# A state-space scan on one core: a\*h split per state, and element-wise work moved from VectorE to GpSimd and ScalarE

## The chip, the cores and the metric

The kernel runs on one core of one Trainium2 chip. The metric is device time in microseconds (us), the median of three runs for the kernel before. A core has five engines that run their own instruction streams in order and meet at semaphores: TensorE (PE, matrix products into the accumulator memory PSUM), VectorE (DVE), ScalarE (ACT, activation functions), GpSimd (POOL) and SyncE (SP, which here issues all DMAs).

## What is computed

The reference, cut to what matters (8 images of 48 x 48 positions, 256 channels, 512 inner channels, 16 states):

```python
xh, z = split(layernorm(x) @ W_in)
xc = depthwise_conv_3x3(xh)
dt_r, Bp, Cp = split(xc @ W_xproj)
dt  = softplus(dt_r @ W_dt + b_dt)          # 512 channels
dtN = dt @ W_dtN + b_dtN                    # 16 states
for t in range(48 * 48):                    # the scan over positions
    dA = exp(dt[t][:, :, None] * A)
    h  = dA * h + (dtN[t] * Bp[t])[:, None, :] * xc[t][:, :, None]
    y[t] = einsum('bdn,bn->bd', h, Cp[t]) + Dskip * xc[t]
y = layernorm(y) * ln_g + ln_b
x = x + (y * silu(z)) @ W_out + b_out
out = x + small_table_function(layernorm(x))   # shifts of 4-bit numbers coded one-hot
```

## The kernel before

The scan has 2304 steps, 48 for each image row, and the state is laid out as 128 partitions (a half of the channels, an image, a pair of states) by 256 channels, twice (the two states n = 0 and 1 of the pair). Of the 256 channels VectorE has 192 (`VD`) and GpSimd 64. A step on VectorE is `decay_state` (L823: one 384-wide product a\*h, both states, in place in PSUM) and then `add_input` (L835: two 192-wide operations, one per state, that add the input and write `h`). ScalarE makes a = exp(dt\*A) for two steps at a time into one of two PSUM buffers (`decay`, L616); it may refill a buffer once the step pair two pairs back is finished, so it leads VectorE by two or three steps. It makes GpSimd's share for four steps at a time (`decay_pool`, L626). Every four steps TensorE sums over the states with the C weights (`sum_states`, L470), for which it needs four finished steps from VectorE and GpSimd; `h` is a ring of eight steps, so VectorE and GpSimd in turn wait for the sum of the quad two quads back.

Around the scan lies a software pipeline over rows. While row i is scanned, row i+1 is convolved and given its dt, row i-1 is normalised, gated, projected and stored, and row i+4 is normalised and projected. The order is written out by hand: the table `SLOT` and conditions on the step `s` (0 to 47) say in which step each stage is issued on each engine, and since every engine runs in order, a stage that waits holds the scan's instructions behind it. The projections share two PSUM banks in strict turn: a stage may use a bank when the stage two turns back has been copied out.

The stages that matter here, with the step at which they stand:

- steps 8 to 12, `dt_project` on TensorE; `softplus_parts`, `softplus_exp`, `softplus_log` on ScalarE (steps 9 to 16); `finish_dt` (L875) on VectorE adds the two parts of softplus (steps 14 to 17).
- steps 9 and 10, `y_log_var` and `y_scale` (L692, L696) on ScalarE make 1/sigma of y, and `y_norm` (L902, three of 512) on VectorE applies it. TensorE transposes y (`yt`), ScalarE scales it (`scale_yn`, L733), VectorE gates it (`gate_y`, L907).
- step 22, `copy_y` (L726) on ScalarE frees `ps_y`; TensorE then runs `add_skip` (L454), a sum, two transposes of dt (L537), `dtn_project` (L544), a sum and `out_project` (L561), whose first result VectorE adds at step 27 (L921).
- steps 33 to 38, z is projected (L496), ScalarE takes tanh(z/2) of it (`gate_tanh`, L741) and VectorE makes z\*(1+tanh(z/2)) = 2 silu(z) (`make_sz`, L914); the factor 2 is taken out of W_out. Behind the last of them stands an explicit load of ScalarE's activation table for exp and ln (L795), and the first tanh has one of its own.
- steps 39 and 40, ScalarE makes 1/sigma for the last norm (L702, L706), for which VectorE waits at step 39 (L943).
- `weigh_c` (L851) spreads the C weights, three times a row, on VectorE; `ln1_apply` (L870) applies the first norm there (steps 20 to 22).

## Time and profile before

| | |
|---|---|
| median of 3 runs | 4378.39 us (4372.62 to 4378.6) |
| the profiled execution | 4383.27 us, span of its instructions 4381.5 us |
| busy: PE, DVE, ACT, POOL | 77%, 91%, 64%, 64% of the span |
| mean granted TensorE clock | 0.815 of full |
| DMA | 78.2% of 16 engines' time, 790 MB |

Busy time is an average over a row whose stretches have different limits. The chain of work that ended last says which engine was being waited for at each moment; the table by windows says how full each engine was between two such moments. An instruction's duration is longer than the time it blocks its engine, since the next may start before the last has drained; where a timeline is at hand, the distance between two starts is the price.

### The profile page before, as it was taken

How to read it: one execution, taken by the hardware profiler on the slowest of the kernel's cores; microseconds unless marked ns; L12 is line 12 of the kernel's file. 1: busy time of each engine (PE TensorE's matmuls, PEld its weight loads, DVE VectorE, ACT ScalarE, POOL GpSimd, SP SyncE). 2: the span in 40 equal slices, each digit the busy share in tenths (PEclk: the TensorE clock that was granted, in tenths of full speed). 3: DMA queues.
4: the chain of work that ended last, by engine and by line, in shares of the span. 5: the costliest groups of instructions: out<-in, count | busy, mean ns of one | idle time of the engine just before them, and what ended most of it. 6: DMA issues, size and time to landing. Idle time of an engine off the chain costs nothing.

```text
span 4381.5 us, 99554 instructions
## 1 busy us (share of the span) xinstructions
PE 3371.7 (77%) x33792; PEld 1640.6 (37%) x33792; DVE 3978.8 (91%) x10877; ACT 2811.1 (64%) x5762; POOL 2797.6 (64%) x5195
## 2 busy tenths in 40 slices
PE   5778787878787777777787878787878787777765
PEld 2334333433343333433343334333433343334322
DVE  2899999999999999999999999999999999999997
ACT  2666666666666666666666666666666666666653
POOL 0766666666666666666666666666666666666664
PEclk8778887888788878888888878887888778878876
DMA  3888788877878787878787888788877878788874
GB/s 71 198 187 191 182 186 185 191 178 183 185 184 186 180 189 182 195 179 188 184 193 177 186 185 189 179 186 187 193 182 183 186 184 186 180 189 182 187 168 105
DMA packets 300420, 789.99 MB, mean 180 GB/s; under 512 B 71301, under 2 KB 225926, under 8 KB 226182
## 3 DMA queue, kind: packets, MB, share of 16 engines
q1 hardware_dynamic: 299910, 783.62, 78.2%
q8 instruction: 268, 4.39, 0.5%
q14 instruction: 242, 1.98, 0.2%
HBM read 648.18 MB, written 96.73 MB: 170 GB/s over the span
## 4 chain that ended last, share of the span: by engine, by line
DVE 47%; PE 31%; ACT 11%; issue 8%; SPq 1%; POOL 1%; DMA 1%; DVEq 0%; ACTq 0%; POOLq 0%
DVE h L835 18%; DVE ps_a L823 13%; PE ps_y L470 6%; PE ps_s L506 6%; ACT ps_a L616 4%; PE ps_y L454 3%; PE ps_s L515 3%; PE ps_s L544 3%; PE ps_s L561 2%; PE ps_s L489 2%; PE ps_s L529 2%; PE ps_s L496 2%; DVE yn L907 2%; DVE res L949 2%; DVE y L902 2%
## 5 line engine op out<-in xcount | busy, mean ns | idle before, releaser
L616 ACT ACTIVATE ps_a<-xb,a_n 128x384 f32<-128x384 f32 x2304 | 1248.0, 574 | 1035.8 <-DVE h L835 1020.9
L835 DVE SCALAR_TENSOR_TENSOR h<-xb,db,ps_a 128x192 f32<-128x192 f32 x4608 | 1685.8, 406 | 62.6 <-DVE ps_a L823 1.4
L1142 POOL TENSOR_TENSOR mp<-ap,h 128x128 f32<-128x128 f32 x2304 | 1091.2, 474 | 520.0 <-ACT ap L626 383.6
L1152 POOL TENSOR_TENSOR h<-mp,up 128x128 f32<-128x128 f32 x2304 | 1108.1, 481 | 489.8 <-PE ps_y L470 305.5
L823 DVE TENSOR_TENSOR ps_a<-ps_a,h 128x384 f32<-128x384 f32 x2304 | 1291.6, 561 | 104.2 <-ACT ps_a L616 12.0
L1132 POOL TENSOR_TENSOR up<-xb,db 128x512 f32<-128x512 f32 x576 | 617.6, 1072 | 532.3 <-DMA xb<-xd 451.1
L470 PE MATMUL ps_y<-h,cw 64*32 64x256 f32 x18432 | 822.3, 478 | 92.9 <-DVE h L835 92.9
L626 ACT ACTIVATE ap<-xb,a_n 128x256 f32<-128x256 f32 x1152 | 519.1, 500 | 171.3 <-DMA xb<-xd 169.8
L470 PEld LDWEIGHTS ps_y<-h,cw 64*32 64x32 f32 x18432 | 322.9, 125 | 528.0 <-issue 259.5
L489 PE MATMUL ps_s<-xlnT,win 128*128 128x384 f32 x768 | 315.9, 550 | 202.1 <-ACT xh L719 152.2
L506 PE MATMUL ps_s<-xs,conv_w 96*32 96x384 f32 x4608 | 411.0, 507 | 13.6 <-ACT xc L634 11.9
L496 PE MATMUL ps_s<-xlnT,win 128*128 128x384 f32 x768 | 325.2, 568 | 117.6 <-DVE sz L914 114.6
L553 PE MATMUL ps_s<-swap,y 128*128 128x128 f32 x576 | 160.7, 434 | 200.6 <-ACT yn L733 169.3
L454 PE MATMUL ps_y<-skip_w,xc 128*32 128x128 f32 x4608 | 197.6, 325 | 136.0 <-ACT y L726 136.0
L561 PE MATMUL ps_s<-wout,yn 128*128 128x256 f32 x1152 | 289.5, 395 | 1.4 <-DVE yn L907 1.4
L529 PE MATMUL ps_s<-xp,wdt 9*128 9x384 f32 x384 | 276.5, 851 | 1.0 <-ACT xp L643 1.0
L489 PEld LDWEIGHTS ps_s<-xlnT,win 128*128 128x128 f32 x768 | 145.4, 204 | 335.8 <-ACT xh L719 204.6
L496 PEld LDWEIGHTS ps_s<-xlnT,win 128*128 128x128 f32 x768 | 155.2, 216 | 268.0 <-DVE sz L914 164.4
L506 PEld LDWEIGHTS ps_s<-xs,conv_w 96*32 96x32 f32 x4608 | 141.5, 114 | 271.2 <-issue 252.7
L561 PEld LDWEIGHTS ps_s<-wout,yn 128*128 128x128 f32 x1152 | 208.7, 191 | 76.2 <-issue 51.6
L454 PEld LDWEIGHTS ps_y<-skip_w,xc 128*32 128x32 f32 x4608 | 145.1, 129 | 198.7 <-ACT y L726 168.1
L553 PEld LDWEIGHTS ps_s<-swap,y 128*128 128x128 f32 x576 | 96.1, 211 | 322.3 <-ACT yn L733 229.2
(107 smaller groups left out, 3799.4 us busy)
## 6 DMA issues: line engine op xcount, KB each, us to landing
xb<-xd SPq DMA_DIRECT2D x576, 1024.0 KB, 7.8
xs<-xh SPq DMA_DIRECT2D x196, 192.0 KB, 8.6
xd<-dttok SPq DMA_DIRECT2D x288, 128.0 KB, 6.1
xin<-in_x_dram SPq DMA_DIRECT2D x144, 128.0 KB, 7.0
xd<-xtok SPq DMA_DIRECT2D x192, 96.0 KB
res<-in_x_dram SPq DMA_DIRECT2D x144, 128.0 KB, 7.1
out_dram<-res SPq DMA_DIRECT2D x144, 128.0 KB, 6.8
xd<-xtok SPq DMA_DIRECT2D x192, 64.0 KB
```

Source lines behind the costliest of these rows:

```text
L470: mm = pe.matmul(ps_y[32 * j:32 * j + 32, half, 0:HALF], weights[part, q * P + 32 * j:q * P + 32 * j + 32], h[part, (4 * Q + j) % HRING, n ...
L489: mm = pe.matmul(bank[:, 0:TOK], win[:, m, c * P:(c + 1) * P], xlnT[:, r % XLN_ROWS, m, :], start=m == 0, stop=m == KM - 1)
L496: mm = pe.matmul(bank[:, 0:TOK], win[:, m, DI + g * P:DI + (g + 1) * P], xlnT[:, r % XLN_ROWS, m, :], start=m == 0, stop=m == KM - 1)
L506: mm = pe.matmul(bank[32 * c:32 * c + 32, 0:TOK], conv_w[0:96, r % 3, dx, NG * c + g, :], xs[0:96, g, c, dx * IMAGES:dx * IMAGES + TOK], s ...
L561: pe.matmul(bank[:, 0:DM], yn[:, g, k * P:(k + 1) * P], wout[:, g, :], start=g == 0, stop=False)
L616: ins = act.activation(ps_a[buf][:, n, 0:2 * VD].rearrange("p (t d) -> p t d", t=2), xb[:, u % XUNITS, 2 * buf:2 * buf + 2, 1, 0:VD], ACT.Exp,
L626: ins = act.activation(ap[:, Q % 2, :, n, :], xb[:, Q % XUNITS, :, 1, VD:HALF], ACT.Exp, scale=a_n[:, n:n + 1])
L823: dve.tensor_tensor(a, a, h[:, (G - 1) % HRING, :, 0:VD], ALU.mult).then_inc(m_done, 1)
L835: ins = dve.scalar_tensor_tensor(h[:, G % HRING, n, 0:VD], xb[:, u % XUNITS, G % 4, 0, 0:VD], db[:, r % 2, n, w:w + 1], ps_a[G // 2 % 2][: ...
L1132: pool.tensor_tensor(up[:, Q % 2], x4, db4.broadcast_to([P, 4, 2, VP]), ALU.mult).then_inc(u_ready, 1)
L1142: pool.tensor_tensor(mp[:, G % 2], ap[:, Q % 2, G % 4], h[:, (G - 1) % HRING, :, VD:HALF], ALU.mult) \
L1152: pool.tensor_tensor(h[:, G % HRING, :, VD:HALF], mp[:, G % 2], up[:, Q % 2, G % 4], ALU.add) \
```

## The change

- **The scan step.** `decay_state` becomes two 192-wide products, each with a semaphore of its own (`m0_done`, `m1_done`), and each of the two adds waits for its own product alone; the next step's first product waits for the first add (`h0_ready`) alone.
- **To GpSimd:** `finish_dt` (two of 768 for four of 384), `weigh_c` and `gate_y`, placed between its scan steps; `gate_y` moves from steps 15 to 19 to steps 19 to 22.
- **To ScalarE:** `y_norm` and `ln1_apply`, as Identity with a per-partition scale and bias. VectorE makes the bias -mean/sigma (`y_shift_by`, `ln1_shift_by`, one small operation each).
- **silu(z)** is made in one ScalarE instruction (`gate_silu`) with the function Silu; `gate_tanh` and `make_sz` go, and so does the halving of W_out.
- The slots of `yt` and `xtok` move to 16 to 19 and 20 to 22.

```diff
 SLOT = {
-    "conv": (0, 1, 3, 4), "xproj": (6,), "dtp": (8, 9, 11, 12), "yt": (14, 15, 16, 18), "xtok": (19, 20, 21),
+    "conv": (0, 1, 3, 4), "xproj": (6,), "dtp": (8, 9, 11, 12), "yt": (16, 17, 18, 19), "xtok": (20, 21, 22),
...
+            def y_norm(r, k):
+                if k == 0:
+                    act.wait_ge(y_shift, r + 1)
+                    act.wait_ge(y_rstd, r + 1)
+                act.activation(y[:, k, :], y[:, k, :], ACT.Identity, bias=nmy[:, k:k + 1],
+                               scale=rsy[:, k:k + 1]).then_inc(y_normed, 1)
...
-            def gate_tanh(r, g):
+            def gate_silu(r, g):
                 act.wait_ge(z_done, r * NG + g + 1)
-                n = r * NG + g
-                if n >= 2:
-                    act.wait_ge(sz_ready, n - 1)
-                act.activation(th[:, n % 2, :], shared_bank("z", r, g)[:, 0:TOK], ACT.Tanh, scale=0.5) \
-                   .then_inc(th_ready, 1)
+                if r >= 1 and g == 0:
+                    act.wait_ge(gated, r * NG)
+                act.activation(sz[:, g, :], shared_bank("z", r, g)[:, 0:TOK], ACT.Silu).then_inc(sz_ready, 1)
...
+                        if s in (12, 13, 14):
+                            y_norm(i - 1, s - 12)
...
+                        if s in (23, 26, 28):
+                            ln1_apply(i + 4, (23, 26, 28).index(s))
...
-                dve.tensor_tensor(a, a, h[:, (G - 1) % HRING, :, 0:VD], ALU.mult).then_inc(m_done, 1)
+                if G >= 1:
+                    dve.wait_ge(h0_ready, G)
+                dve.tensor_tensor(a[:, 0], a[:, 0], last[:, 0], ALU.mult).then_inc(m0_done, 1)
+                if G >= 1:
+                    dve.wait_ge(h_ready, G)
+                dve.tensor_tensor(a[:, 1], a[:, 1], last[:, 1], ALU.mult).then_inc(m1_done, 1)
...
+            def finish_dt(r, half):
+                pool.wait_ge(sp_log, r * 2 + half + 1)
+                part = dt[:, 2 * half:2 * half + 2, :].rearrange("p g t -> p (g t)")
+                pool.tensor_tensor(part, part, dttok[:, 2 * half * TOK:(2 * half + 2) * TOK], ALU.add).then_inc(dt_ready, 1)
+
+            def gate_y(r, g):
+                pool.wait_ge(yn_ready, r * NG + g + 1)
+                pool.wait_ge(sz_ready, r * NG + g + 1)
+                pool.tensor_tensor(yn[:, g, :], yn[:, g, :], sz[:, g, :], ALU.mult).then_inc(gated, 1)
...
+                    if s in (16, 17) and exists(i + 1):
+                        finish_dt(i + 1, s - 16)
+                    if s in (10, 27) and exists(i):
+                        weigh_c(i * KT + s // 16 + 1)
+                    if s == 43 and exists(i + 1):
+                        weigh_c((i + 1) * KT)
+                    if s in (19, 20, 21, 22) and exists(i - 1):
+                        gate_y(i - 1, s - 19)
```

The kernel's text doesn't name the loads of ScalarE's tables but for two; the compiler adds the rest. The order of ScalarE's instructions from the first gate of a row (step 34) on, before: `th` is the tanh, `ap` and `ps_a` are the exponentials of the scan.

```order
L741 ACT_TABLE_LOAD [waits sz_ready]
L741 ACTIVATE th<-ps_s1 128x384 [waits z_done]
L626 ACTIVATE ap<-xb,a_n 128x4x64 [waits hp_ready,x_loaded0]
L626 ACTIVATE ap<-xb,a_n 128x4x64
L741 ACTIVATE th<-ps_s0 128x384 [waits sz_ready,z_done]
L616 ACTIVATE ps_a0<-xb,a_n 128x384 [waits h_ready,x_loaded0]
L616 ACTIVATE ps_a0<-xb,a_n 128x384
L741 ACTIVATE th<-ps_s1 128x384 [waits sz_ready,z_done]
```

The same place after the change, where `sz` is the silu:

```order
L758 ACT_TABLE_LOAD [waits gated]
L758 ACTIVATE sz<-ps_s1 128x384 [waits z_done]
L630 ACT_TABLE_LOAD [waits hp_ready]
L630 ACTIVATE ap<-xb,a_n 128x4x64 [waits x_loaded0]
L630 ACTIVATE ap<-xb,a_n 128x4x64
L758 ACT_TABLE_LOAD
L758 ACTIVATE sz<-ps_s0 128x384 [waits z_done]
L620 ACT_TABLE_LOAD [waits h_ready]
L620 ACTIVATE ps_a0<-xb,a_n 128x384 [waits x_loaded0]
L620 ACTIVATE ps_a0<-xb,a_n 128x384
L758 ACT_TABLE_LOAD
```

Each exponential that stands between two gates has got a table load ahead of it, and each gate too. In the whole program the loads go from 97 to 385, 6 more for each of the 48 rows: before, two a row (the first tanh, L795); after, eight, all between steps 34 and 38.

VectorE in a step with no other work (steps 2 and 3 of a row), before:

```order
L823 TENSOR_TENSOR ps_a1<-ps_a1,h 128x2x192 [waits h_ready,a_ready]
L835 SCALAR_TENSOR_TENSOR h<-xb,db,ps_a1 128x192 [waits m_done]
L835 SCALAR_TENSOR_TENSOR h<-xb,db,ps_a1 128x192
L823 TENSOR_TENSOR ps_a1<-ps_a1,h 128x2x192 [waits h_ready]
L835 SCALAR_TENSOR_TENSOR h<-xb,db,ps_a1 128x192 [waits m_done]
```

And in such steps after:

```order
L845 TENSOR_TENSOR ps_a1<-ps_a1,h 128x192 [waits h0_ready,a_ready]
L848 TENSOR_TENSOR ps_a1<-ps_a1,h 128x192 [waits h_ready]
L861 SCALAR_TENSOR_TENSOR h<-xb,db,ps_a1 128x192 [waits m0_done]
L864 SCALAR_TENSOR_TENSOR h<-xb,db,ps_a1 128x192 [waits m1_done]
L845 TENSOR_TENSOR ps_a1<-ps_a1,h 128x192 [waits h0_ready]
```

Four instructions stand where three stood, and between any of them and the one it waits for there is now another.

## Rows read from the trace of the kernel before

**Rows 1.** The page: span and busy time of each engine.

```profile
span 4381.5 us, 99554 instructions
PE 3371.7 (77%) x33792; PEld 1640.6 (37%) x33792; DVE 3978.8 (91%) x10877; ACT 2811.1 (64%) x5762; POOL 2797.6 (64%) x5195
```

**Rows 2.** The page: the chain that ended last, shares by engine.

```profile
DVE 47%; PE 31%; ACT 11%; issue 8%; SPq 1%; POOL 1%; DMA 1%; DVEq 0%; ACTq 0%; POOLq 0%
```

**Rows 3.** Six windows of one row: length, busy us of engines, PEclk, DMA share, GB/s.

```profile
2004.63:2016.97 12.34, 12.29 (x123) 6.99 (x124) 9.48 (x24) 6.25 (x13) 7.20 (x15) 0.75 0.70 177
2016.97:2024.67 7.70, 7.70 (x58) 4.86 (x59) 7.36 (x20) 2.97 (x7) 3.84 (x8) 1.00 1.04 282
2024.67:2037.23 12.56, 8.06 (x114) 4.11 (x112) 11.79 (x33) 11.06 (x22) 8.10 (x17) 1.00 0.89 196
2037.23:2045.70 8.47, 5.63 (x46) 2.61 (x44) 8.47 (x27) 3.03 (x8) 7.44 (x15) 1.00 0.57 131
2045.70:2070.20 24.50, 22.34 (x250) 8.35 (x258) 22.74 (x70) 17.04 (x38) 15.03 (x30) 0.90 0.75 171
2070.20:2093.76 23.56, 13.88 (x126) 7.00 (x110) 23.05 (x57) 18.15 (x39) 16.59 (x28) 0.57 0.89 181
```

**Rows 4.** The chain in order of time, behind a copy of y: start, us, what.

```profile
2004.68 1.94 PE ps_y L454 x32
2006.62 1.89 PE ps_y L470 x32
2008.51 1.90 PE ps_s L537 x8
...
2016.97 0.42 DVE res L921
```

**Rows 5.** Timeline of DVE in steps without other work: start, us, engine, line, operation.

```profile
2010.74 0.57 DVE L823 TENSOR_TENSOR ps_a<-ps_a,h 128x384 f32<-128x384 f32 x1
2011.34 0.74 DVE L835 SCALAR_TENSOR_TENSOR h<-xb,db,ps_a 128x192 f32<-128x192 f32 x2
2012.18 0.57 DVE L823 TENSOR_TENSOR ps_a<-ps_a,h 128x384 f32<-128x384 f32 x1
```

**Rows 6.** Timeline of ACT through the gates, steps 34 to 39.

```profile
2024.67 1.09 ACT L616 ACTIVATE ps_a<-xb,a_n 128x384 f32<-128x384 f32 x2 [1.92 <-DVE h L835]
2025.77 1.28 ACT L741 ACT_TABLE_LOAD   x1
...
2028.33 0.47 ACT L741 ACTIVATE th<-ps_s 128x384 f32<-128x384 f32 x1
2028.69 1.07 ACT L616 ACTIVATE ps_a<-xb,a_n 128x384 f32<-128x384 f32 x2
...
2033.20 0.47 ACT L741 ACTIVATE th<-ps_s 128x384 f32<-128x384 f32 x1
2033.69 1.28 ACT L795 ACT_TABLE_LOAD   x1
2034.99 0.91 ACT L626 ACTIVATE ap<-xb,a_n 128x256 f32<-128x256 f32 x2
```

**Rows 7.** Groups of instructions, DVE and ACT: busy us, mean ns, idle before, releasers.

```profile
L835 DVE SCALAR_TENSOR_TENSOR h<-xb,db,ps_a 128x192 f32<-128x192 f32 x4608 | 1685.8, 406 | 62.6 <-DVE ps_a L823 1.4 <-issue 0.5
L902 DVE TENSOR_SCALAR y<-y,mvy,rsy 128x512 f32<-128x512 f32 x144 | 96.9, 674 | 32.9 <-ACT rsy L696 31.9
L733 ACT ACTIVATE yn<-ps_s,bet,gam 128x384 f32<-128x384 f32 x192 | 125.5, 656 | 2.8 <-PE ps_s L553 2.8
L741 ACT ACTIVATE th<-ps_s 128x384 f32<-128x384 f32 x192 | 92.7, 483 | 46.9 <-PE ps_s L496 46.2
L726 ACT ACTIVATE y<-ps_y 128x512 f32<-128x512 f32 x144 | 83.5, 580 | 6.9 <-PE ps_y L470 6.9
```

**Rows 8.** Groups of instructions on POOL, the same columns.

```profile
L1142 POOL TENSOR_TENSOR mp<-ap,h 128x128 f32<-128x128 f32 x2304 | 1091.2, 474 | 520.0 <-ACT ap L626 383.6
L1132 POOL TENSOR_TENSOR up<-xb,db 128x512 f32<-128x512 f32 x576 | 617.6, 1072 | 532.3 <-DMA xb<-xd 451.1 <-issue 79.3 <-POOL h L1152 0.3
```

More of the change, by code:

```diff
@@ L897, in y_aggregate, with y_shift_by @@
                 ins.then_inc(y_var, 1)
-            def y_norm(r, k):
-                if k == 0:
-                    dve.wait_ge(y_rstd, r + 1)
-                dve.tensor_scalar(y[:, k, :], y[:, k, :], mvy[:, k, 0:1], rsy[:, k:k + 1], ALU.subtract, ALU.mult) \
-                   .then_inc(y_normed, 1)
-            def gate_y(r, g):
-                dve.wait_ge(yn_ready, r * NG + g + 1)
-                dve.tensor_tensor(yn[:, g, :], yn[:, g, :], sz[:, g, :], ALU.mult).then_inc(gated, 1)
-            def make_sz(r, g):
-                dve.wait_ge(th_ready, r * NG + g + 1)
-                if r >= 1 and g == 0:
-                    dve.wait_ge(gated, r * NG)
-                dve.scalar_tensor_tensor(sz[:, g, :], th[:, (r * NG + g) % 2, :], 1.0,
-                                         shared_bank("z", r, g)[:, 0:TOK], ALU.add, ALU.mult).then_inc(sz_ready, 1)
+            def y_shift_by(r):
+                dve.wait_ge(y_rstd, r + 1)
+                if r >= 1:
+                    dve.wait_ge(y_normed, r * KT)
+                dve.scalar_tensor_tensor(nmy[:], mvy[:, :, 0], -1.0, rsy[:], ALU.mult, ALU.mult).then_inc(y_shift, 1)
             def add_residual(r, k):
@@ L1012, in middle @@
                     if s == 9:
-                        y_norm(i - 1, 0)
-                    if s == 10:
-                        y_norm(i - 1, 2)
-                    if s in (15, 16, 18, 19):
-                        gate_y(i - 1, (15, 16, 18, 19).index(s))
+                        y_shift_by(i - 1)
                     if s in (27, 29, 30):
@@ L1030, in middle @@
                         y_stats(i * KT + s // 16 - 1)
-                    if s in (34, 35, 37, 38):
-                        make_sz(i, (34, 35, 37, 38).index(s))
                 if exists(i + 1):
@@ L1048, in after @@
                         y_aggregate(i - 1)
-                    if s == 9:
-                        y_norm(i - 1, 1)
                     if s == 33:
@@ L1153, in pool_add, with weigh_c @@
                     .then_inc(hp_ready, 1)
+            def weigh_c(third):
+                r, k = third // KT, third % KT
+                if k == 0:
+                    pool.wait_ge(states_loaded, (r + 1) * 4 * SEM_DMA)
+                if third >= 2:
+                    pool.wait_ge(c_done, 4 * (third - 1))
+                for n in range(2):
+                    dst = cw[:, third % 2, n, :, 0:P].rearrange("p q (j f) -> p q j f", f=32)[:, :, :, 0:IMAGES]
+                    c = cs[:, r % 2, n, k * THIRD:(k + 1) * THIRD].rearrange("p (q j) -> p q j", j=4)
+                    ins = pool.tensor_tensor(dst, c.unsqueeze(3).broadcast_to([P, 4, 4, IMAGES]),
+                                             mod8[:].unsqueeze(1).unsqueeze(1).broadcast_to([P, 4, 4, IMAGES]), ALU.mult)
+                ins.then_inc(cw_ready, 1)
+            def finish_dt(r, half):
[6 more added lines that the diff above has]
+                pool.tensor_tensor(yn[:, g, :], yn[:, g, :], sz[:, g, :], ALU.mult).then_inc(gated, 1)
             pool.memset(ident[:], 0.0).then_inc(ident_set, 1)
```

99 lines of the change are left out of this document (45 added, 54 removed).

## The prediction, made before the changed kernel ran

> **What bounds the kernel now.** The page first [rows 1]: VectorE is busy 91% of the span, so one would say that VectorE is the limit and that whatever leaves it is won. The chain that ended last says otherwise [rows 2]: only 47% of it lies on VectorE, 31% on TensorE and 11% on ScalarE. So I followed the chain in order of time through one row and cut the row where the chain changes engine, then asked for the busy times in those windows [rows 3]. Six pieces make a row of 89.1 us:
>
> - A, 2045.70 to 2070.20, 24.5 us: TensorE busy for 22.3. ScalarE's copies let the last projection start, then the convolution, x_project and dt_project run without a gap, and ScalarE makes 1/sigma of y behind the second dt_project.
> - B, 2070.20 to 2093.76, 23.56 us: VectorE busy for 23.05. It carries y_norm, finish_dt and gate_y beside the scan; ScalarE is busy for 18.15 and otherwise waits for it. It ends with copy_y.
> - C, 2004.63 to 2016.97, 12.34 us: TensorE busy for 12.29, from add_skip to the first out_project; VectorE waits for it with the residual [rows 4].
> - D, 2016.97 to 2024.67, 7.70 us: TensorE busy all of it (the other out_projects), VectorE nearly so.
> - E, 2024.67 to 2037.23, 12.56 us: the gates, steps 34 to 39. VectorE 11.79, ScalarE 11.06. It ends where ScalarE delivers 1/sigma for the last norm.
> - F, 2037.23 to 2045.70, 8.47 us: VectorE busy all of it.
>
> Only B, E and F have VectorE near its limit. What VectorE loses in A, C and D can't shorten them, as long as TensorE's list there is the same.
>
> **The scan step.** Now a bare step takes 2012.18 - 2010.74 = 1.44 us [rows 5]: 0.60 from the product to the adds, 0.84 from there to the next product. The two adds together take 0.74 and one takes 0.406 [rows 7], so they start 0.33 apart; the rest is waiting for one's own result. After the split every dependent pair has an instruction in between. A 192-wide product in PSUM isn't in the trace: below, half of the 384-wide one, 0.28; above, an add of the same width, 0.33. I take 0.28, as the product reads one operand less. A bare step is then 2 x 0.28 + 2 x 0.33 = 1.22 us, 0.22 less. Where another operation already stands between product and adds the wait was hidden, and the gain is near nothing. Against the split speaks the Trainium skill, "VectorE: DVE Perf Modes", section on the TRN2 errata: a fixed cost is paid per instruction, so many small tiles pay it many times. By the formula of that section for a PSUM source, four 192-wide operations are an estimated 1.30 us a step, which would touch piece F by some 0.3 us. In this case's rows the wait removed is larger than the fixed cost added: 0.84 us from adds to product, against 0.66 of work of the two adds, and 0.60 from product to adds [rows 5].
>
> **Piece B.** VectorE loses y_norm (three of 0.67, [rows 7]), finish_dt, gate_y and a weigh_c, and gets 0.1 us for the shift. Its part is then some 13 bare steps (15.9 us) with the first norm's statistics (about 1.4), 17.3. ScalarE becomes the longer one. It has 18.15 busy now [rows 3]. It gets three y_norms: a 512-wide copy takes 580 ns, and the pair of per-partition operands adds 656 - 483 = 173 [rows 7], 0.75 as a duration, 0.65 from start to start (0.47 long, 0.36 apart in [rows 6]): +1.95. The third copy of xtok (0.48) moves behind copy_y. Sum 19.6. Then two smaller things: with yt and xtok moved later, a sum over states at half clock (1.89, [rows 4]) stands ahead of the first xtok, for which I add 0.6, and the first transpose of dt now waits for ScalarE's step 22 and pushes add_skip by 0.3. B goes from 23.56 to 20.5: **-3.1 us**. Bounds: -4.2 (nothing waits) to -1.5 (each of the three y_norms costs 0.5 more than taken).
>
> **Piece C.** The same TensorE list. Its first three entries run at half clock (PEclk 0.75 in the window, 5.7 us of entries at 0.5 level; [rows 3, 4]) because TensorE idled before. With B shorter it idles less, and part of the 5.7 us may run at full clock, 2.4 us less at the most, as dttok must also wait for ScalarE. I take **-0.7** of 0 to -2.4.
>
> **Piece E.** This is where the change costs. With Silu the exponentials between the gates need another table than the gates, and the order shows 8 loads a row for 2. A load is 1.28 long, 2034.99 - 2033.69 = 1.30 to the next instruction, and the one ahead of it must drain: 0.49 from tanh to load against 0.36 from tanh to exponential, and 1.10 for the pair before the first load [rows 6]. So 1.39 us each, six more are 8.3 us. All lie between the decay of step 34, which waits for VectorE's step 31, and the ln and exp of steps 39 and 40, for which VectorE waits at step 39; each exponential among them is a decay for which VectorE also waits (step 36, step 38). ScalarE's 11.06 busy [rows 3] becomes 19.4, with no idle left, since TensorE's z and VectorE's steps are early by then. That replaces 12.56: **+6.8 us**. Bounds: +6.0 (Silu and overlaps kinder) to +8.5 (waits in between remain, as 1.5 now). The make_sz that VectorE loses (four of 0.54 long) is worth nothing here, for VectorE now waits.
>
> For the price of a load the Trainium skill, "ScalarE: Activation LUTs", section "What ACT_TABLE_LOAD costs", has 1283 ns plus a drain of about 1380, 2.66 us for every switch. The trace agrees with the first and shows 0.1 in place of the second [rows 6].
>
> **Pieces A, D, F.** A and D: TensorE's list is unchanged, 0. In A the start may shift: TensorE idles during the gates now, so that its clock may be half where it was full (up to +1), or its late projections close the gap before the last one (down to -1). F: the statistics-and-table work of VectorE is unchanged; 0 within 0.3.
>
> **GpSimd** gets, per row, two 768-wide adds (474 ns for 128 and 1072 for 512 [rows 8], so 1.47 each), four 384-wide products (0.87 each), three pairs of weigh_c (about 0.6 to 0.9): 8.5 us on 58. Of these 6.4 fall on steps 16 to 22, in B. There it has 16.59 busy [rows 3] and would have 23.6 in 20.5 us, so it falls behind; it may, by one quad: the sum that needs its step 23 stands behind 8.7 us of TensorE's list in C, where GpSimd has 5 us free. I find it ready some 3 us ahead. Its cover is no more than that. DMA, at 0.89 in B, would be at some 0.97 with the same bytes in 20.5 us; ScalarE's loads there had about 1 us to spare.
>
> **Sum.** -3.1 - 0.7 + 6.8 = +3.0 us a row, 48 rows: +144. On the profiled execution's 4383.3: 4527, and that execution lay 5 us above the median. Forecast **4525 us**, +3.3%.
>
> **Rivals.**
> 1. *TensorE's clock pays for the tables* (faster). If C runs at full clock from its start (-2.4), B gets its whole -4.2, and A starts its last projection and its first sum at full clock (-1.5), a row is 1.6 below now with E at +6.5: 4383 - 77 = 4306. It decides when B, C and A together give back more than E's +6.8. For it: half clock in B and C follows idling, and B gets denser. Against it: all three must come together. 0.12; some 0.06 more for sums that end within 0.2% (about what a measurement of this kernel can tell from no change).
> 2. *GpSimd becomes the bound in B and C* (slower still): if its added operations wait for VectorE's memory accesses or the order costs 3 us more than the cover, +3 a row more: 4670. 0.10.
> 3. *Every switch costs twice what the load lasts*: the engine stands empty as long again (1.28) around each of the six new loads, +7.7 a row more, 4895. The two loads of a row now show 0.1 [rows 6], which speaks against it. 0.03. The drain that the Trainium skill names in "ScalarE: Activation LUTs" would be this rival.
> 4. *The change does what the page's 91% suggests*: VectorE's freed time comes off, and the loads hide. ScalarE has 12.56 - 11.06 = 1.5 us of idle in E against 8.3 of loads, so they can't. It is within the chance of the first.
>
> The forecast's own case has 0.69, with 4440 to 4610 by the bounds of B, C and E together. The range for 8 in 10 reaches a little to both sides: 4400 to 4650. Faster 0.13, same 0.06, slower 0.81.
>
> **What would show it.** 384 table loads of 1.28 us within the row loop, 8 a row; the window from the decay of step 34 to VectorE's L938 (`hot`) at 19 us; VectorE's busy share down to some 70% with waits for ScalarE's `ps_a` in steps 34 to 38, which it hardly has now; bare steps of 1.22; from 1/sigma to copy_y 20 us with ScalarE full. It would be wrong if `ps_y` or `h` of GpSimd were what VectorE waits for, or if the bare step is not below 1.35.

## The result, and the profile after

| | before | after |
|---|---|---|
| median | 4375.51 us (4371.78 to 4378.6) | 4624.62 us (4610.95 to 4632.56, four runs) |
| ratio, 95% interval | 1 | 1.0561, 1.054 to 1.0582 |
| span of the profiled execution | 4381.5 us | 4616.9 us |
| mean granted TensorE clock | 0.815 | 0.804 |

The change makes the kernel 5.6% slower. The forecast was 4525 us, 3.3% slower, with a range from 4400 to 4650. Sign and main mechanism were right, but 4624.62 lies above the 4440 to 4610 of the forecast's own case, and about 100 us were missed. The first experiments go after these.

The page of after: its span, the busy times, and the shares of the chain that ended last, by engine and by line (against [rows 1] and [rows 2]).

```profile
span 4616.9 us, 102146 instructions
PE 3404.6 (74%) x33792; PEld 1659.1 (36%) x33792; DVE 3476.1 (75%) x12124; ACT 3340.9 (72%) x6338; POOL 3140.4 (68%) x5771
ACT 32%; DVE 16%; PE 16%; DMA 15%; SPq 13%; issue 7%; POOL 1%; ACTq 0%; POOLq 0%; DVEq 0%
DMA xb<-xd 14%; ACT ps_a L620 8%; SPq L351 8%; ACT L758 4%; PE ps_y L474 4%; SPq L361 4%; ACT ap L630 3%; PE ps_s L510 3%; DVE h L861 3%; ACT L620 3%; DVE h L864 2%; DVE ps_a L845 2%; PE ps_s L519 2%; ACT dt L680 2%; DVE ps_a L848 2%
```

VectorE's busy share fell from 91% to 75%, and its share of the chain from 47% to 16%. Two things took its place. ScalarE (11% to 32%) was expected. DMA with 15% and SyncE's queue with 13%, 1% each before, were not: the transfers of the scan's input (`xb<-xd`) and the SyncE lines L351 and L361 are now part of the path that sets the end.

The same windows for a row of after, in the order C, D, E, (F left out), A, B. Columns as in [rows 3]: length, busy us of PE, PEld, DVE, ACT, POOL, granted clock, DMA share, GB/s.

```profile
2197.79:2208.14 10.35, 9.95 (x126) 5.48 (x125) 6.94 (x21) 8.01 (x17) 9.48 (x19) 1.00 0.44 115
2208.14:2217.41 9.27, 9.27 (x84) 5.63 (x92) 6.87 (x22) 2.91 (x6) 6.79 (x14) 1.00 0.97 247
2217.41:2237.43 20.02, 9.55 (x102) 4.46 (x86) 9.93 (x37) 19.13 (x29) 9.71 (x20) 0.74 0.68 148
...
2245.75:2271.28 25.53, 23.37 (x250) 8.90 (x258) 21.77 (x83) 16.75 (x36) 15.48 (x31) 0.84 0.81 187
2271.28:2292.07 20.79, 13.44 (x125) 6.98 (x112) 18.35 (x63) 19.59 (x41) 16.65 (x26) 0.54 0.97 206
```

A single row is a sample, so I took the distance between the same six marks in every row from 4 to 43 of a trace, and the mean over these 40 rows. All later tables are made this way:

| us | A | B | C | D | E | F | row |
|---|---|---|---|---|---|---|---|
| before | 24.83 | 23.01 | 11.89 | 7.77 | 12.72 | 8.32 | 88.54 |
| after | 24.41 | 20.47 | 10.38 | 9.50 | 20.36 | 8.02 | 93.14 |
| measured difference | -0.4 | -2.5 | -1.5 | +1.7 | +7.6 | -0.3 | +4.6 |
| forecast | 0 | -3.1 | -0.7 | 0 | +6.8 | 0 | +3.0 |

48 times 4.6 is 221 us of the 235 by which the span grew; the rest lies in the first and last rows. Two pieces carry the miss: D, which should not have moved, and E, 0.8 us over its term. The forecast started from a single row of 89.1 us, whose B is 23.56 and whose C is 12.34; the 40 rows have 23.01 and 11.89 on average.

**Where E goes.** ScalarE through the gates of after (start, us, what; against [rows 6]):

```profile
2218.50 1.28 ACT L758 ACT_TABLE_LOAD   x1
2219.79 0.49 ACT L758 ACTIVATE sz<-ps_s 128x384 f32<-128x384 f32 x1
2220.30 1.28 ACT L630 ACT_TABLE_LOAD   x1
2222.26 0.91 ACT L630 ACTIVATE ap<-xb,a_n 128x256 f32<-128x256 f32 x2 [0.67 <-DMA xb<-xd]
2223.18 1.28 ACT L758 ACT_TABLE_LOAD   x1
2224.47 0.49 ACT L758 ACTIVATE sz<-ps_s 128x384 f32<-128x384 f32 x1
```

Of the 6.46 us from 2218.50 to the end of the second silu at 2224.96, 3.84 are loads. Each is 1.28 long and the next instruction starts 1.29 after its start, unless it waits: at 2222.26 the exponential has waited 0.67 us more, for a transfer of `xb`. That wait was not in the forecast.

**Where D goes.** The chain in order of time, from the first out_project of C to the gates (start, us, what). L351 is `store_x`, twelve DMAs that SyncE issues, L361 is `store_dt`, six of them, and L375 issues the load of a unit, which is the scan's input for four steps.

```profile
2197.79 0.79 ACT ap L630 x2
2198.58 0.50 ACT xtok L655
...
2199.09 0.85 SPq L351
...
2206.85 0.77 SPq L351
...
2207.72 0.57 SPq L375
...
2208.47 0.59 SPq L361
...
2212.08 0.61 SPq L361
...
2212.79 9.44 DMA xb<-xd
```

The copies of `xtok` on ScalarE now end here, one step later in the program. Relative to VectorE's step 24 the last of them ends 1.5 us ahead, where it ended 5.1 us ahead before (medians over the rows). SyncE waits for them with `store_x`, then spends 2199.09 to 2207.6 on issuing twelve stores, and only then does it issue the load of unit 8 (steps 32 to 35). Six stores of dt stand ahead of the load of unit 9, which then takes 9.44 us and lands at 2222.2: the 0.67 us wait above. What the late load of unit 8 does stands in the timeline of ScalarE in D, and in that of VectorE behind it:

```profile
2209.25 1.08 ACT L620 ACTIVATE ps_a<-xb,a_n 128x384 f32<-128x384 f32 x2 [3.45 <-DVE h L864]
2215.59 0.91 ACT L630 ACTIVATE ap<-xb,a_n 128x256 f32<-128x256 f32 x2 [5.25 <-DMA xb<-xd]
```

```profile
2217.50 0.37 DVE L845 TENSOR_TENSOR ps_a<-ps_a,h 128x192 f32<-128x192 f32 x1 [1.76 <-ACT ps_a L620]
```

ScalarE stands still for 5.25 us until the input is there, makes the exponentials for step 32 and those behind it, and VectorE waits 1.76 us for them. That is the growth of D: TensorE's out_projects are no longer what ends it.

The waits of after, over the whole span (engine, line waited for: us in total, times, longest):

```profile
POOL mp L1120 <- ACT ap L630: 598.3, 184, 7.7
DVE ps_a L845 <- ACT ps_a L620: 577.6, 355, 19.6
ACT ap L630 <- DMA xb<-xd: 370.4, 157, 7.7
```

VectorE waits 577.6 us for `ps_a`, 12 us a row, where the forecast had put such waits without a size; ScalarE's `ap` waits 370.4 us for transfers, 169.8 before. SyncE's own wait for the copies of `xtok`, before and then after:

```profile
SPq L347 <- ACT xtok L651: 58.1, 48, 13.1
```

```profile
SPq L351 <- ACT xtok L655: 251.6, 48, 13.1
```

That is 4.0 us a row more. Issuing the twelve stores takes 8.5 us in both kernels, so the load of unit 8 goes out 7.2 us behind the start of VectorE's step 24, where it went out 3.5 us behind before. From issue to landing it takes 7.9 us in both.

**Smaller readings.** A bare step of VectorE (start, us, engine, line, operation; against [rows 5]):

```profile
2201.75 0.36 DVE L845 TENSOR_TENSOR ps_a<-ps_a,h 128x192 f32<-128x192 f32 x1
2202.01 0.35 DVE L848 TENSOR_TENSOR ps_a<-ps_a,h 128x192 f32<-128x192 f32 x1
...
2202.60 0.41 DVE L864 SCALAR_TENSOR_TENSOR h<-xb,db,ps_a 128x192 f32<-128x192 f32 x1
2202.93 0.35 DVE L845 TENSOR_TENSOR ps_a<-ps_a,h 128x192 f32<-128x192 f32 x1
```

It takes 2202.93 - 2201.75 = 1.18 us, where 1.44 stood before. And the groups of the operations that moved, with one group of loads (busy us, mean ns, idle before; against [rows 7] and [rows 8]):

```profile
L758 ACT ACT_TABLE_LOAD x192 | 246.3, 1283 | 3.4
L703 ACT ACTIVATE y<-y,nmy,rsy 128x512 f32<-128x512 f32 x144 | 116.7, 812 | 0.2 <-DVE nmy L910 0.2
L1155 POOL TENSOR_TENSOR yn<-yn,sz 128x384 f32<-128x384 f32 x192 | 192.6, 1004 | 16.6 <-ACT yn L751 16.6
L1150 POOL TENSOR_TENSOR dt<-dt,dttok 128x768 f32<-128x768 f32 x96 | 173.9, 1811 | 85.6 <-ACT dt L680 85.6
```

### The profile page after: what moved, and what is told of

It is laid out like the page before. It is cut to its first block, busy times and chain, and to the rows that moved or that the text cites. A ratio compares the mean times of both kernels' runs of the same rounds, so it can differ in the third digit from the quotient of the medians.

```text
span 4616.9 us, 102146 instructions
## 1 busy us (share of the span) xinstructions
PE 3404.6 (74%) x33792; PEld 1659.1 (36%) x33792; DVE 3476.1 (75%) x12124; ACT 3340.9 (72%) x6338; POOL 3140.4 (68%) x5771
## 4 chain that ended last, share of the span: by engine, by line
ACT 32%; DVE 16%; PE 16%; DMA 15%; SPq 13%; issue 7%; POOL 1%; ACTq 0%; POOLq 0%; DVEq 0%
DMA xb<-xd 14%; ACT ps_a L620 8%; SPq L351 8%; ACT L758 4%; PE ps_y L474 4%; SPq L361 4%; ACT ap L630 3%; PE ps_s L510 3%; DVE h L861 3%; ACT L620 3%; DVE h L864 2%; DVE ps_a L845 2%; PE ps_s L519 2%; ACT dt L680 2%; DVE ps_a L848 2%
## 5 line engine op out<-in xcount | busy, mean ns | idle before, releaser
L1120 POOL TENSOR_TENSOR mp<-ap,h 128x128 f32<-128x128 f32 x2304 | 1050.9, 456 | 712.5 <-ACT ap L630 598.3
L1130 POOL TENSOR_TENSOR h<-mp,up 128x128 f32<-128x128 f32 x2304 | 1056.1, 458 | 321.3 <-PE ps_y L474 108.1
L845 DVE TENSOR_TENSOR ps_a<-ps_a,h 128x192 f32<-128x192 f32 x2304 | 817.2, 355 | 585.1 <-ACT ps_a L620 577.6
L864 DVE SCALAR_TENSOR_TENSOR h<-xb,db,ps_a 128x192 f32<-128x192 f32 x2304 | 929.6, 403 | 0.0
L861 DVE SCALAR_TENSOR_TENSOR h<-xb,db,ps_a 128x192 f32<-128x192 f32 x2304 | 922.7, 400 | 2.7 <-PE ps_y L474 0.6
L474 PE MATMUL ps_y<-h,cw 64*32 64x256 f32 x18432 | 795.1, 464 | 136.7 <-DVE h L864 132.6
L848 DVE TENSOR_TENSOR ps_a<-ps_a,h 128x192 f32<-128x192 f32 x2304 | 809.7, 351 | 0.0
L630 ACT ACTIVATE ap<-xb,a_n 128x256 f32<-128x256 f32 x1152 | 521.0, 503 | 376.2 <-DMA xb<-xd 370.4
L500 PE MATMUL ps_s<-xlnT,win 128*128 128x384 f32 x768 | 358.6, 609 | 270.0 <-ACT sz L758 270.0
L493 PE MATMUL ps_s<-xlnT,win 128*128 128x384 f32 x768 | 363.6, 620 | 169.2 <-ACT xh L737 91.8
L510 PE MATMUL ps_s<-xs,conv_w 96*32 96x384 f32 x4608 | 397.9, 494 | 24.4 <-ACT xh L737 13.8
L500 PEld LDWEIGHTS ps_s<-xlnT,win 128*128 128x128 f32 x768 | 157.2, 221 | 434.7 <-ACT sz L758 335.4
L493 PEld LDWEIGHTS ps_s<-xlnT,win 128*128 128x128 f32 x768 | 167.2, 233 | 326.7 <-ACT xh L737 127.1
L758 ACT ACT_TABLE_LOAD x192 | 246.3, 1283 | 3.4
L510 PEld LDWEIGHTS ps_s<-xs,conv_w 96*32 96x32 f32 x4608 | 152.6, 111 | 250.2 <-issue 220.9
```

The lines of the kernel that those rows point to most:

```text
L474: mm = pe.matmul(ps_y[32 * j:32 * j + 32, half, 0:HALF], weights[part, q * P + 32 * j:q * P + 32 * j + 32], h[part, (4 * Q + j) % HRING, n ...
L493: mm = pe.matmul(bank[:, 0:TOK], win[:, m, c * P:(c + 1) * P], xlnT[:, r % XLN_ROWS, m, :], start=m == 0, stop=m == KM - 1)
L510: mm = pe.matmul(bank[32 * c:32 * c + 32, 0:TOK], conv_w[0:96, r % 3, dx, NG * c + g, :], xs[0:96, g, c, dx * IMAGES:dx * IMAGES + TOK], s ...
L630: ins = act.activation(ap[:, Q % 2, :, n, :], xb[:, Q % XUNITS, :, 1, VD:HALF], ACT.Exp, scale=a_n[:, n:n + 1])
L845: dve.tensor_tensor(a[:, 0], a[:, 0], last[:, 0], ALU.mult).then_inc(m0_done, 1)
L848: dve.tensor_tensor(a[:, 1], a[:, 1], last[:, 1], ALU.mult).then_inc(m1_done, 1)
```

## The experiments

The theory after the result: six table loads a row are worth about 6.7 us of E, and the rest of the growth in D and E (some 2.8 us a row) is SyncE's queue, where stores hold the scan's loads. The rivals: that Silu itself, or the order of work around it, costs the time, and not the loads; that the late transfers come from DMA bandwidth, and not from the order of the queue; that VectorE or GpSimd is what waits. A second question is what the split and each of the moves are worth once the loads are gone.

### 1. The tanh form put back

After, with the four tanh on ScalarE and `make_sz` on VectorE as before; every other part of the change stays. The loads return to two a row.

```diff
-            def gate_silu(r, g):
+            def gate_tanh(r, g):
...
+                    if s in (34, 35, 37, 38):
+                        make_sz(i, (34, 35, 37, 38).index(s))
...
+                    dve.tensor_scalar(wout[:], wout[:], 0.5, None, ALU.mult)
```

> The changed kernel with one part undone: the gate is again tanh on ScalarE and the product on VectorE, so that two table loads a row stand where eight stood. Theory (the six added loads are the loss, all of them on the path in the stretch of the gates): that stretch goes from 20.4 us back to about 12.7, a row from 93.1 to 85.5, 4255 us, clearly below the kernel before. Rival (the loads mostly hide, and the loss comes from the work moved to GpSimd and ScalarE or from the split): 4560 or more.

Measured 4346.27 us, 0.9917 of before (0.9896 to 0.9937): 278 us below after, but 91 above the expectation. E falls to 13.91, D stays at 9.61, where before has 12.72 and 7.77. The page of this kernel says what is left, in the chain by engine and in the group of ScalarE's exponentials for GpSimd:

```profile
PE 30%; ACT 25%; DVE 15%; SPq 12%; DMA 10%; issue 7%; POOL 1%; ACTq 0%; POOLq 0%; DVEq 0%
L632 ACT ACTIVATE ap<-xb,a_n 128x256 f32<-128x256 f32 x1152 | 520.9, 503 | 407.3 <-DMA xb<-xd 403.9
```

SyncE's queue and DMA still hold 22% of the chain, and ScalarE waits 403.9 us for transfers. So the late loads of the input don't come from the table loads; they are a second cost.

### 2. Silu alone on the kernel before

```diff
-                act.activation(th[:, n % 2, :], shared_bank("z", r, g)[:, 0:TOK], ACT.Tanh, scale=0.5) \
-                   .then_inc(th_ready, 1)
+                act.activation(sz[:, g, :], shared_bank("z", r, g)[:, 0:TOK], ACT.Silu).then_inc(sz_ready, 1)
...
-                    if s in (34, 35, 37, 38):
-                        make_sz(i, (34, 35, 37, 38).index(s))
```

> The kernel before with one part alone: Silu in one ScalarE instruction, make_sz gone, eight table loads a row. Theory: +7.6 us a row in the stretch of the gates, 48 rows, 4375 + 365 = 4740. Rival (ScalarE idles for 36% of the span, so loads hide): 4450 or less.

Measured 4695.29 us, 1.0722 (1.0707 to 1.0738), the slowest kernel of all. E is 19.45 instead of 12.72, +6.7, and every other piece is within 0.4 of before. This is the term of the forecast (+6.8) by itself: 6.7 x 48 = 323 us of the 320 measured. The run's own expectation, +7.6 a row and 4740, was 45 us too high: it took all of the growth of E for the loads. VectorE is spared four operations a row here and gains nothing from it.

### 3. The loads without Silu

The kernel of experiment 1 with six useless switches a row, placed where the compiler places them with Silu. Nothing is left out of the computation; the loads are added.

```diff
+                        if s in (35, 36, 38):
+                            act.preload_act_table_set("exp_and_others")
...
+                        if s in (35, 37, 38):
+                            act.preload_act_table_set("exp_and_others")
```

> t_tanh with six table loads a row put in by hand at the places where the compiler put them for Silu; nothing needs them. Theory (it is the loads, not the function or the missing product on VectorE): within 40 us of the changed kernel, 4625. Rival (Silu's own speed, or the order of bank releases, is the cost): within 60 us of t_tanh.

Measured 4613.4 us, 1.0535 (1.0517 to 1.0552), against 4624.62 for after; E is 20.24 against 20.36. The groups of the added loads in this kernel:

```profile
L776 ACT ACT_TABLE_LOAD x144 | 184.8, 1283 | 2.5
L817 ACT ACT_TABLE_LOAD x144 | 184.8, 1283 | 2.6
```

With the loads and no Silu, E comes out within 0.12 us of after. The rival that Silu itself is the cost falls. The idle time ahead of the loads is 2.5 us for 144, 17 ns each, so a switch costs little more than its 1283 ns. The Trainium skill, "ScalarE: Activation LUTs", section "What ACT_TABLE_LOAD costs", gives the same 1283 ns and a drain of some 1380 besides; the first agrees with these rows, the second doesn't show in them. Had it been there, six loads would cost an estimated 16 us a row.

### 4. The stores of x behind the load of unit 8

After, with one number of SyncE's list changed:

```diff
-                    if s == 21 and exists(i + 1):
+                    if s == 24 and exists(i + 1):
                         store_x(i + 1)
```

> The changed kernel with one edit in SyncE's order: the twelve stores of x stand behind the load of unit 8 (step 24) and not ahead of it (step 21). Theory (the growth of the stretch behind the first out_project from 7.8 to 9.5 us is SyncE's: the load waits behind twelve stores that wait for the later xtok copies): that stretch comes back to about 7.9, 48 x 1.6, 4545 us. Rival (ScalarE's backlog alone makes VectorE wait there): 4610 or more. A second rival: the stores, now later, push the load of unit 9, and the wait only moves by four steps: 4600 to 4640.

Measured 4557.42 us, 1.0403 (1.0386 to 1.042). D is 7.64 instead of 9.50; E stays at 20.71 (20.36), since the stores of dt still stand ahead of the load of unit 9. 67 us come from the order of one queue alone. That the transfers lacked bandwidth is ruled out for D: from issue to landing the load of unit 8 takes 7.9 us in after, 7.9 in before and 7.6 here, and what moved is its issue, from 7.2 us behind step 24 to 0.7 ahead of it. For unit 9 both count: in after it is issued 3.7 us late and takes 9.8 us, and with the stores of dt behind it (experiment 9) 0.1 us late and 7.9.

### 5. Both stores behind the loads, with tanh

The kernel of experiment 1, with two numbers of SyncE's list changed:

```diff
-                    if s == 21 and exists(i + 1):
+                    if s == 24 and exists(i + 1):
                         store_x(i + 1)
-                    if s == 26 and exists(i + 1):
+                    if s == 28 and exists(i + 1):
                         store_dt(i + 1)
```

> t_tanh with both groups of stores on SyncE behind the next load: the stores of x at step 24 and those of dt at step 28, each after the load of unit 8 and 9. Theory (late loads of units 8 and 9 are what is left of the loss, in the stretch behind the first out_project and in that of the gates): those two stretches come back from 9.6 and 13.9 to 7.7 and 12.8 us, a row from 87.9 to 84.9, 4200 us. Rival (ScalarE's extra work makes them long): 4300 or more.

Measured 4169.59 us, 0.9522 (0.9506 to 0.9538): 177 us below experiment 1 and 4.8% below the kernel before. D is 7.64 and E is 12.50. Its chain by engine and the same group as in experiment 1:

```profile
PE 38%; ACT 26%; DVE 25%; issue 7%; DMA 2%; SPq 1%; POOL 1%; ACTq 0%; POOLq 0%; DVEq 0%
L632 ACT ACTIVATE ap<-xb,a_n 128x256 f32<-128x256 f32 x1152 | 520.0, 502 | 51.4 <-DMA xb<-xd 47.5
```

ScalarE's wait for transfers falls from 403.9 to 47.5 us, and DMA with SyncE's queue from 22% of the chain to 3%. The load of unit 8 is issued 0.7 us before VectorE starts step 24 (median over the rows) instead of 7.2 us behind it; in the kernel before it was 3.5 us behind.

### 6. The split taken out again

The kernel of experiment 5 with one 384-wide product a\*h for the two 192-wide ones, as before.

```diff
-                dve.tensor_tensor(a[:, 0], a[:, 0], last[:, 0], ALU.mult).then_inc(m0_done, 1)
...
-                dve.tensor_tensor(a[:, 1], a[:, 1], last[:, 1], ALU.mult).then_inc(m1_done, 1)
+                dve.tensor_tensor(a, a, h[:, (G - 1) % HRING, :, 0:VD], ALU.mult).then_inc(m0_done, 1)
```

> t_sp2 with the scan step as in the kernel before: one 384-wide product, then both adds. Theory (with ScalarE and TensorE on the path, the 0.26 us that a bare step gains is worth little): 4225 us, 25 above t_sp2. Rival (the split is the main gain of the change): 0.22 x 26 bare steps x 48 rows = 275 us above t_sp2, 4475.

Measured 4200.7 us, 0.9596 (0.9575 to 0.9618). The split is worth 31 us here, 0.7%, spread over E (+0.33 without it), B (+0.13) and C (+0.11). A bare step is 0.26 us shorter with it, and 48 of those would be 12.5 us a row; 0.6 arrives.

### 7. The split alone on the kernel before

> The kernel before with one part alone: the product and the adds split per state and interleaved. Theory: it pays only where VectorE is the limit and steps are bare, a few steps in the stretch from 1/sigma to copy_y and in that of the gates, about 1.2 us a row, 4320 us. Rival (every bare step pays): 0.26 x 20 bare steps x 48 rows, 4130 us. Third: nothing, 4375.

The edit is the first bullet of the change and nothing else. Measured 4368.87 us (ten runs), 0.9982 (0.997 to 0.9994), where 4320 was expected: nearly nothing. Bare steps are 1.18 us, but B is 22.96 (23.01 before). The waits of VectorE in the kernel before, and then in this one, where L902 has become L910, L921 L929 and L943 L951:

```profile
DVE res L921 <- PE ps_s L562: 76.5, 50, 4.4
DVE y L902 <- ACT rsy L696: 31.9, 35, 2.0
DVE hot L943 <- ACT rs L706: 20.2, 26, 1.6
```

```profile
DVE y L910 <- ACT rsy L698: 117.4, 47, 2.8
DVE res L929 <- PE ps_s L564: 94.3, 64, 5.1
DVE hot L951 <- ACT rs L708: 54.6, 48, 1.4
```

These three waits grow from 128.6 to 266.3 us, 2.9 us a row. What VectorE saves in its steps it spends on waiting, at the fixed places where TensorE or ScalarE deliver: for 1/sigma of y at step 9, for the residual at step 27, for `hot` at step 39. The lengths of the steps, from one first product to the next (us, mean over the 40 rows), show both sides:

| us | 0 to 5 | 9 | 10 to 22 | 26 and 27 | 36 | 39 |
|---|---|---|---|---|---|---|
| before | 8.66 | 3.08 | 24.01 | 5.80 | 1.48 | 5.52 |
| split alone | 7.41 | 4.95 | 23.47 | 6.64 | 1.18 | 6.22 |

Steps 0 to 5, nearly all bare, save 1.3 us, and step 9, the wait for 1/sigma at the end of A, takes 1.9 more. B gets little because it has hardly a bare step: between product and adds, or behind them, most of steps 10 to 22 hold another operation, which had hidden the wait already. Steps 13 and 14 get 0.25 us shorter each, but step 16 goes from 2.49 to 2.61 and step 18 from 1.72 to 1.91.

### 8. y_norm back on VectorE

The kernel of experiment 5, with `y_norm` as a tensor_scalar on VectorE at steps 9 and 10, as before.

```diff
-                        if s in (12, 13, 14):
-                            y_norm(i - 1, s - 12)
...
-                        y_shift_by(i - 1)
+                        y_norm(i - 1, 0)
```

> t_sp2 with y_norm back on VectorE, at its old steps 9 and 10, as one operation with two per-partition operands; ScalarE has 2 us less a row. Theory (ScalarE sets the stretch from 1/sigma to copy_y, and VectorE has 2 us of room there): that stretch from 20.5 to about 19.3, 4145 us. Rival (the stretch is set by VectorE or GpSimd by now): 4200 or more, as t_sp2.

Measured 4162.12 us, 0.9502 (0.9486 to 0.9518), the fastest kernel here, though its interval overlaps that of experiment 5. B is 19.95 instead of 20.54, where 19.3 was expected. ScalarE is the longer engine in B, so the one move of the change that went to ScalarE's side there cost a little, which A (+0.2) and the rest in part give back.

### 9. Both stores behind the loads, with Silu

After with the two edits of experiment 5.

> The changed kernel with both groups of SyncE stores behind the next load, Silu kept. Theory (losses add: six table loads are worth 6.7 us a row, as in b_silu, on top of t_sp2): 4170 + 48 x 6.7 = 4490; against a_spmove it takes the 1.1 us a row that a late load of unit 9 adds to the stretch of the gates. Rival (unit 9 hides behind the table loads, which make ScalarE late anyway): 4557, as a_spmove.

Measured 4535.78 us, 1.035 (1.0318 to 1.0382). D is 7.64 and E is 19.37, the forecast's value for E (19.4), 1.0 below after. The whole was expected at 4490, experiment 5 and 6.7 us a row, and is 46 us above, since A came out at 25.74 where experiment 5 has 24.58 (1.16 x 48 = 56 us). Its chain by engine:

```profile
ACT 39%; PE 38%; DVE 14%; issue 6%; SPq 1%; DMA 1%; POOL 1%; ACTq 0%; POOLq 0%
```

SyncE and DMA have left it, and ScalarE has 39% with its loads. Row by row, A takes few values, near 23.7, 24.6 and 25.8 in experiment 5; here it is 25.7 or more in 37 of 40 rows. They go with TensorE's clock (see the end).

### 10. Both stores behind the loads, on the kernel before

> The kernel before with the same two moves in SyncE's order. Theory (the late loads bound nothing before: unit 8 is issued 3.5 us late there too, but VectorE comes later): within 25 us of the kernel before, 4380. Rival (the late load cost time before too, so that it is no part of this change's loss): 4330 or less.

Measured 4438.4 us, 1.0119 (1.0071 to 1.0168): slower by 60 us where no change was expected. The transfers are early here too. The timelines of GpSimd and of VectorE in step 27 (start, us, engine, line, operation) show what came in their place:

```profile
2042.05 0.46 POOL L1152 TENSOR_TENSOR h<-mp,up 128x128 f32<-128x128 f32 x1
2042.46 1.11 POOL L1132 TENSOR_TENSOR up<-xb,db 128x512 f32<-128x512 f32 x1
```

```profile
2041.63 0.73 DVE L835 SCALAR_TENSOR_TENSOR h<-xb,db,ps_a 128x192 f32<-128x192 f32 x2
2042.28 1.44 DVE L851 TENSOR_TENSOR cw<-cs,mod 128x128 f32<-128x128 f32 x2
2043.64 0.55 DVE L823 TENSOR_TENSOR ps_a<-ps_a,h 128x384 f32<-128x384 f32 x1
```

With its input there earlier, GpSimd runs `up` (1.11 us) just while VectorE makes the C weights. The pair takes 1.44 us; the second of it lasts 1.14 us where this operation otherwise takes 275 to 279 ns, and it ends at 2043.72, just behind GpSimd's operation (2043.57). The durations of this operation (minimum, median, maximum ns), in the kernel before and in this one:

```profile
L851 DVE TENSOR_TENSOR cw<-cs,mod x288: 275/279/1153, 108.4 to 4311.3; 128x128 f32<-128x128 f32 x144
```

```profile
L851 DVE TENSOR_TENSOR cw<-cs,mod x288: 276/368/1161, 107.8 to 4370.0; 128x128 f32<-128x128 f32 x144
```

The median went from 279 to 368. Of the 288, 68 are longer than 430 ns, 55 of them beside GpSimd's `up`; in the kernel before it was 27, 6 of them beside `up`. D is 0.8 longer, which is what one such operation a row costs, and E 0.5.

### 11. GpSimd's share given back to VectorE

The kernel of experiment 5 with `finish_dt`, `gate_y` and `weigh_c` on VectorE, at the same steps.

> t_sp2 with finish_dt, gate_y and weigh_c on VectorE, at the same steps; y_norm stays on ScalarE. Theory (what GpSimd took is what shortened the stretch from 1/sigma to copy_y, and through it the idling of TensorE): that stretch from 20.5 to 22 or more, 4245 us or more. Rival (ScalarE sets that stretch either way): within 20 us of t_sp2, 4170.

Measured 4245.73 us, 0.9679 (0.9645 to 0.9713). The time is near the one expected, but not by the way expected: B was to be 22 or more, with VectorE full, and is 20.70. The loss is C (+0.4) and E (+0.65). Its chain by engine:

```profile
DVE 34%; PE 22%; ACT 20%; DMA 10%; SPq 7%; issue 6%; POOL 0%; ACTq 0%; DVEq 0%; POOLq 0%
```

VectorE carries more of it, as it should, but so do DMA (10%, 2% in experiment 5) and SyncE (7%, 1%); the loads of units 9 to 11 are issued 2.2 to 2.8 us late. The trace says how: VectorE gets from step 24 to step 28 in 7.2 us here (8.6 in experiment 5), but the twelve stores that stand between the loads of units 8 and 9 take 8.5 us to issue. So GpSimd's share is worth 76 us in this setting, and the mechanism that I had given for it in B fell: B is 20.5 to 20.7 in every kernel with `y_norm` on ScalarE, whoever has GpSimd's share, and 19.95 in experiment 8. So neither move is needed for the short B: each was undone, and it stayed. `ln1_apply` and the new slots, the other edits that touch B, were not tried alone.

### 12. The C weights on GpSimd, on top of experiment 10

The kernel of experiment 10 with `weigh_c` on GpSimd, behind its scan step, and nothing else.

> b_sp2 with one edit: weigh_c runs on GpSimd, between its scan steps, and not on VectorE. In b_sp2 the second operation of weigh_c in step 27 takes 1142 ns where it takes 278 in the kernel before, and it ends with the 1.06 us operation of GpSimd that runs meanwhile, since the load that GpSimd waits for now lands earlier. Theory (VectorE's operation with two inputs in SBUF stands still while GpSimd's long one runs): without weigh_c on VectorE the stretch behind the first out_project comes from 8.6 back to 7.7 us, and the kernel to 4438 - 48 x 0.9 = 4395 or below. Rival (the earlier load or the later stores slow the row in another way, DMA or SyncE): 4425 or more.

Measured 4391.13 us (ten runs), 1.0025 (1.0015 to 1.0034). D is 7.70 and E is 12.74, as in the kernel before, so 47 of the 60 us of experiment 10 came from this one operation that stood still beside GpSimd's. The two operations can't collide when they stand in one engine's line. The remaining 12 us go with B, which is 23.25 where experiment 10 has 22.89; why isn't shown.

The pieces of all twelve, mean over 40 rows:

| us | A | B | C | D | E | F | row |
|---|---|---|---|---|---|---|---|
| 1 tanh form | 25.09 | 20.54 | 10.35 | 9.61 | 13.91 | 8.35 | 87.87 |
| 2 Silu alone | 25.09 | 22.98 | 11.77 | 7.78 | 19.45 | 7.96 | 95.04 |
| 3 loads, no Silu | 24.29 | 20.46 | 10.35 | 9.65 | 20.24 | 8.03 | 93.03 |
| 4 one store moved | 24.58 | 20.50 | 10.35 | 7.64 | 20.71 | 8.09 | 91.87 |
| 5 tanh, both moved | 24.58 | 20.54 | 10.35 | 7.64 | 12.50 | 8.28 | 83.89 |
| 6 without split | 24.56 | 20.67 | 10.46 | 7.69 | 12.83 | 8.27 | 84.48 |
| 7 split alone | 25.30 | 22.96 | 11.51 | 7.64 | 12.89 | 8.35 | 88.66 |
| 8 y_norm on VectorE | 24.78 | 19.95 | 10.40 | 7.63 | 12.47 | 8.38 | 83.61 |
| 9 Silu, both moved | 25.74 | 20.56 | 10.35 | 7.64 | 19.37 | 8.31 | 91.98 |
| 10 before, both moved | 24.86 | 22.89 | 11.98 | 8.57 | 13.20 | 8.15 | 89.65 |
| 11 shares on VectorE | 24.63 | 20.70 | 10.76 | 7.72 | 13.15 | 8.19 | 85.16 |
| 12 as 10, C weights moved | 24.62 | 23.25 | 11.99 | 7.70 | 12.74 | 8.27 | 88.57 |

## Why the prediction was right, and where it was off

- **Piece E, right.** Forecast +6.8 from six loads of 1.39 us that nothing can hide. Experiment 2 gives +6.7 for Silu alone, experiment 3 the same E with loads and no Silu, and experiment 9 gives 19.37 for a forecast of 19.4. The measured +7.6 is that and 1.0 from the late load of unit 9.
- **Piece D, the step that failed.** "TensorE's list is unchanged, 0". The list was, and D grew by 1.7 all the same. The forecast followed the copies of `xtok` on ScalarE and TensorE, and not to SyncE, which waits for them with twelve stores ahead of the load that step 32 needs. The trace of before already showed the danger (SyncE's issues of `store_x` hold the load of unit 8 until 3.5 us behind step 24), and of late loads the forecast said only, for B, that "ScalarE's loads there had about 1 us to spare". Experiments 4 and 9 show D back at 7.64. By pieces, the 1.6 us a row by which the sum fell short (+4.6 for +3.0) are D 1.7, E 0.8 and B 0.6, less C 0.8, A 0.4 and F 0.3; the queue is all of the first and, by experiment 9, all of the second.
- **Piece B, right** (-2.5 for -3.1). The forecast's length for it was 20.5 us and the mean is 20.47; the 0.6 us lie in the starting point, a row with a B of 23.56 where the mean is 23.01. ScalarE was busy for 19.59 of 20.79 us, 19.6 in the forecast's sum. Its `y_norm` took 812 ns, not 750; experiment 8 puts the three of them at 0.6 us of B.
- **Piece C, more than taken** (-1.5 for -0.7, inside 0 to -2.4). The window stands at a granted clock of 1.00, the upper of the two levels (2.4 GHz), where it had 0.75 before: before, TensorE came to it from idle time in B at the lower level (1.2 GHz), and now from a B that is 2.5 us shorter with the same list. The clock accounts for the size: in the kernel before, C lasts 11.2 us in the rows with 2.8 us at the lower level and 12.35 in those with 6.1, and a line through its 40 rows gives 10.4 us at none, which is what after has with 0.06 us. That the shorter B is the cause is a reading: the five kernels with a B near 23 us have 3.5 to 4.8 us at the lower level in C, the nine with 20 to 20.7 have 0.5 or less, but no experiment isolates it. Rival 1 counted on this and on two others together; this one came, B's full -4.2 and A's -1.5 didn't.
- **Pieces A and F, right** (-0.4 and -0.3, within the 1 and 0.3 given). The +1 that A's bound allowed came in experiment 9 (25.74, +0.9), not here.
- **The bare step.** 1.22 forecast, 1.18 measured, and 1.30 by the estimate from the Trainium skill's formula, "VectorE: DVE Perf Modes", TRN2 errata. The row decides against the last, and against the rule's warning for this change: the waits removed are larger than the fixed cost of one more instruction. That the gain is nearly nothing in time (experiments 6 and 7) has another reason: the time comes back as waits at steps 9, 27 and 39.
- **GpSimd.** Its operations were undersized: 1.81 us for the 768-wide add (forecast 1.47) and 1.00 for the 384-wide product (0.87), 1.2 us a row more. The cover held: TensorE waited for GpSimd's `h` once in the whole span, for 2.7 us. Rival 2 did not happen.
- **Rivals 3 and 4.** A switch costs 1.29 to 1.30 us, not twice that. VectorE's share came off the page (91% to 75%, 70 forecast) and not off the time.
- **The sum.** +3.0 a row became +4.6, and 4525 became 4624.62. The range held it by luck: the forecast's own case ended at 4610, and only the margin added on both sides reached 4650. No term and no rival had the queue.

What the change could have been worth: without Silu and with SyncE's two numbers changed it is 0.9522 of before, where it was 1.0561. One function and two numbers turned a gain of 4.8% into a loss of 5.6%: 278 us by the table loads (after against experiment 1) and 177 us by the queue (experiment 1 against 5). The split of the 455 us depends on the order: taken the other way round it is 89 us for the queue (after against experiment 9) and 366 for the loads (experiment 9 against 5). Of the 206 us by which experiment 5 is below before, the split has 31, GpSimd's share 76 and `y_norm` -7; the rest, some 100 us, was not taken apart.

## What to carry to other kernels

Before swapping two activations for one fused one, look which functions stand between its uses on the same engine: each alternation is a table load at full price, and it counts when the engine has no idle time to pay from. When a step is moved or made later, follow it into every queue that waits for it, the one that only issues DMAs too, and read what stands behind that wait; here the transfer held back belonged to another stage altogether. And a saving on an engine that is 91% busy is worth only what the places where it meets the others let through.
